# Loading a two-layer megakernel in six waited groups, and moving five pieces of its steady loop

## The reference

```python
# layer 0, on the normalised input
favor:   q, k, v = x@Wq, x@Wk, x@Wv        # 16 heads of 8, 32 random features each
         phi = exp(x @ proj.T - |x|^2/2); causal linear attention; out = num / den
local:   2 blocks of: q, k = l2norm(h@wqkv) * scale, rotary; windowed softmax(q k^T) v; x += o @ wo
         then h = layernorm(shift(x)); x += (a * gelu(g)) @ w2 + b2
# layer 1
attention: 16 heads of 8, softmax(q k^T) v
moe:       top 2 of 8 experts plus a shared one, silu(x@W3) * (x@W1) @ W2
```

## Time and profile before

| | |
|---|---|
| median of 3 runs | 2192.03 us (2189.34 to 2197.23) |
| the profiled execution | 2193.24 us |
| its span in the trace | 2191.5 us |
| mean granted TensorE clock | 0.952 of full |
| first DMA issued / first projection of turn 0 | 8.06 us / 76.48 us |

### The profile page before, as it was taken

One profiled execution on the slowest core, in us unless ns is written; L12 is line 12 of the kernel. 1 busy time (PEld: TensorE's weight loads), 2 busy tenths in 40 slices (PEclk: granted clock), 3 DMA queues, 4 the chain that ended last, 5 costly groups with the idle time before them and its releaser, 6 DMA issues.

```text
span 2191.5 us, 43331 instructions
## 1 busy us (share of the span) xinstructions
PE 1835.0 (84%) x18116; PEld 1061.8 (48%) x18116; DVE 1335.9 (61%) x2752; ACT 765.2 (35%) x1441; POOL 272.2 (12%) x222
## 2 busy tenths in 40 slices
PE   1698898988988889878888888888897988988887
PEld 1254454554544644536445454454553554545544
DVE  1567546765476745767547675476656675467754
ACT  0323433324533235323352232623425223433234
POOL 0101101101021010110210102101011011012010
PEclk9999999999999989999999999999999999999999
DMA  4000200002000020000200001000100002000010
GB/s 177 1 7 2 28 4 6 6 2 30 2 11 1 2 29 6 8 1 2 29 7 7 1 9 23 7 7 1 19 14 6 7 2 29 2 6 1 3 29 7
DMA packets 27477, 29.77 MB, mean 14 GB/s; under 512 B 3525, under 2 KB 25845, under 8 KB 26741
## 3 DMA queue, kind: packets, MB, share of 16 engines
q1 hardware_dynamic: 27284, 27.01, 6.3%
HBM read 12.06 MB, written 2.36 MB: 7 GB/s over the span
## 4 chain that ended last, share of the span: by engine, by line
PE 52%; DVE 28%; ACT 7%; issue 5%; DMA 4%; SPq 4%; POOL 0%; ACTq 0%; DVEq 0%
PE bank L957 5%; PE bank L731 5%; PE bank L947 4%; PE bank L932 4%; DMA phi<-parts 3%; SPq L430 3%; DVE ls L1455 3%; DVE ftm L1381 2%; PE bank L763 2%; PE bank L970 2%; ACT phi L1246 2%; DVE lc L1437 2%; ACT lc L1246 2%; PE bank L669 2%; DVE parts L1391 2%
## 5 line engine op out<-in xcount | busy, mean ns | idle before, releaser
L1622 DVE TENSOR_REDUCE amx<-bank 128x2 f32<-128x512 f32 x256 | 163.1, 685 | 98.4 <-PE bank L970 98.4
L1212 ACT ACTIVATE silu<-bank 128x512 f32<-128x512 f32 x144 | 84.1, 595 | 298.0 <-PE bank L932 286.0
L1610 DVE TENSOR_TENSOR mh<-bank,silu 128x512 f32<-128x512 f32 x144 | 99.5, 692 | 123.4 <-PE bank L947 115.1
L957 PEld LDWEIGHTS bank<-w_mw,mh 128*128 128x128 f32 x1152 | 145.2, 202 | 24.4 <-issue 24.4
L957 PE MATMUL bank<-w_mw,mh 128*128 128x128 f32 x1152 | 153.2, 289 | 0.0
L1641 DVE RECIPROCAL ftm<-bank 128x512 f32<-128x512 f32 x16 | 53.7, 3358 | 154.4 <-PE bank L1053 154.4
L485 POOL TENSOR_TENSOR xB<-xn2T,lsq 128x512 f32<-128x512 f32 x32 | 40.7, 1273 | 812.1 <-ACT lsq L1218 812.1
L932 PE MATMUL bank<-xn2T,w_mw 128*128 128x512 f32 x288 | 141.1, 612 | 0.0
L1455 DVE RECIPROCAL ls<-bank 128x256 f32<-128x256 f32 x64 | 112.2, 1753 | 39.7 <-PE bank L783 39.6
L1443 DVE TENSOR_REDUCE lmx<-bank 128x4 f32<-128x512 f32 x128 | 79.5, 685 | 89.4 <-PE bank L731 89.4
L669 PE MATMUL bank<-hT,w_wqkv 128*128 128x512 f32 x256 | 119.0, 602 | 11.9 <-ACT lsq L1123 6.2
(11 more groups left out here) (284 smaller groups left out, 3678.1 us busy)
## 6 DMA issues: line engine op xcount, KB each, us to landing
phi<-parts SPq DMA_DIRECT2D x96, 64.0 KB
lc<-parts SPq DMA_DIRECT2D x96, 64.0 KB
w_mw<-in_mw SPq DMA_DIRECT2D x3, 1152.0 KB
x_in<-in_x SPq DMA_DIRECT2D x8, 256.0 KB, 2.7
out<-res SPq DMA_DIRECT2D x8, 256.0 KB, 2.3
w_wqkv<-in_wqkv SPq DMA_DIRECT2D x1, 1536.0 KB
w_w<-in_w SPq DMA_DIRECT2D x1, 682.0 KB
mh<-in_rotary SPq DMA_DIRECT2D x1, 512.0 KB
```

The source lines that it names most:

```text
L957: last = mm(bank_of("final")[:, t], mh[:, (2 * q + i) % 4, t], W["mw2"][:, ORDER[q], i, :], start=(q == 0 and j == 0 and i == 0), stop=Fal ...
L1610: V.tensor_tensor(mh[:, n % 4, :], bank_of("moe_u", n)[:], silu[:, n % 2, :], ALU.mult).then_inc(sem["moe_h"], 1)
L1622: V.tensor_reduce(amx[:, 2 * b:2 * b + 2, h], bank_of("att_max", n)[:].rearrange("p (t k) -> p t k", t=2), AX.X, ALU.max).then_inc(sem["at ...
```

## The change

1. SP issues x_in first and then the weights in six groups (LOADS), each with a semaphore of its own; each engine waits for a group where it first needs it. wqkv is loaded in two halves. The 116 first increments go from SP to ACT, in reversed order, and ACT loads its Exp table then. POOL waits for nothing. DVE normalises the first input before it prepares the tables, and PE transposes it before the bias products.
2. EARLY = 3: early values 0 and 1 are computed right after the next turn's input is transposed, early value 2 after the attention's values. In l = 0 only values(3) is left in the turn. In l = 1 values(0) moves in front of sums(0).
3. Quad 7 of the favor attention moves from (1, "raws") to (1, "sums"), its values from (1, "sums") to (1, "nmT").
4. The maxima are dealt out later: pairs 0 and 1 both after expert_out(2), and so on; the last place has one pair instead of two.
5. The centring of l = 0 uses the matrix `center` (identity less 1/128) in place of the mean, ACT squares the bank, and DVE copies it to cen after the square.
6. The denominators of sequence 1: PE multiplies the sums as stationary operand with an 8-column selector (den8), so that they stand transposed in 32 columns; DVE takes 128 x 32 reciprocals, copies them out 16-fold, PE turns them back with four products against the identity (`att_rows`), and DVE multiplies from the bank.

```diff
+LOADS = {
+    "first": ("ident", "cols"),
+    "gated": ("w1", "b1", "center"),
+    "favor": ("fw", "aw", "block8", "projT"),
+    "local": ("rotary", "wqkv0", "rows"),
+    "tables": ("sumrow", "causal", "sumcol", "ident4", "headrow", "winmask", "nmrow", "bandmask", "den", "den8", "mean"),
+    "rest": ("wo", "w2", "wqkv1", "wr", "rb", "pick", "rank", "mw3", "mw1", "mw2"),
 }
...
-        EARLY = 2
+        EARLY = 3
-                    (0, "mean"): 4, (0, "var"): 5, (0, "gain"): 6, (1, "raws"): 7}
+                    (0, "mean"): 4, (0, "var"): 5, (0, "gain"): 6, (1, "sums"): 7}
-                    (0, "var"): 4, (0, "gain"): 5, (0, "out"): 6, (1, "sums"): 7}
+                    (0, "var"): 4, (0, "gain"): 5, (0, "out"): 6, (1, "nmT"): 7}
-        MAX_AT = {3: ((), (0,), (1, 2)), 4: ((3,), (4,), (5,)), 5: ((6,), (7,), (8,)),
-                  6: ((9,), (10,), (11,)), 7: ((12,), (13,), (14, 15))}
+        MAX_AT = {3: ((), (), (0, 1)), 4: ((2,), (3,), (4, 5)), 5: ((6,), (7,), (8,)),
+                  6: ((9,), (10,), (11, 12)), 7: ((13,), (14,), (15,))}
...
         def _(sp):
-            for n in COUNTS:
-                sp.sem_inc(sem[n], COUNTS[n])
+            sp.dma_start(x_in[:], x[0]).then_inc(x_in_sem, 16)
+            for group, names in LOADS.items():
+                for n in names:
...
         def _(pool):
-            pool.wait_ge(loaded, 16 * N_LOADS)
...
+            pe.wait_ge(started, 9)
+            pe.wait_ge(*arrived("first"))
             turn_input(0)
+            bias_products()
             pe.wait_ge(sem["xnT"], COUNTS["xnT"] + 1)
+            pe.wait_ge(*arrived("local"))
             for j in range(EARLY):
                 early_value(0, j)
             pe.wait_ge(sem["loc_v"], COUNTS["loc_v"] + EARLY)
             for i in range(2):
                 favor_query(0, i)
             pe.wait_ge(sem["favor_qk"], COUNTS["favor_qk"] + 2)
+            centred_weights()
             favor_values(0)
+            pe.wait_ge(prep, 13)
+            pe.wait_ge(*arrived("tables"))
...
                         if p == 2:
+                            if l:
+                                values(0)
                             sums(0)
...
                     sums(1)
-                    values(2)
+                    if l:
+                        values(2)
...
-                        mm(o[:], W["mean"][:], h, start=True, stop=True).then_inc(sem["glu_mean_ps"], 1)
+                        mm(o[:], W["center"][:], h, start=True, stop=True).then_inc(sem["glu_mean_ps"], 1)
...
                 if it + 1 < TURNS:
                     turn_input(it + 1)
-                    early_value(it + 1, 0)
+                    for j in range(2):
+                        early_value(it + 1, j)
...
+                        for i in range(4):
+                            last = mm(bank_of("att_pv", b)[:, 8 * i:8 * i + 8], heads[:, b, i * P:(i + 1) * P], W["den8"][:],
+                                      start=True, stop=True)
+                        last.then_inc(sem["att_den"], 1)
+
+                def att_rows():
+                    pe.wait_ge(sem["att_rec"], now("att_rec", 2))
+                    for i in range(4):
+                        last = mm(bank_of("att_pv", 1)[:, i * P:(i + 1) * P], ftm[:, i, :], I[:], start=True, stop=True)
+                    last.then_inc(sem["att_rows_ps"], 1)
...
                 if it + 1 < TURNS:
                     favor_values(it + 1)
-                else:
+                att_rows()
+                if it + 1 == TURNS:
                     att_project(it, 1)
...
         def _(act):
-            act.wait_ge(prep, 14)
+            for n in reversed(COUNTS):
+                act.sem_inc(sem[n], COUNTS[n])
             act.wait_ge(started, 9)
+            A(warm[:], phibias[:], ACT.Exp)
...
+                        if l == 1 and c == 5:
+                            local_value(0)
...
-                        act.wait_ge(sem["glu_cen"], now("glu_cen", l + 1))
-                        A(csq, cen[:], ACT.Square).then_inc(sem["glu_sq"], 1)
+                        act.wait_ge(sem["glu_mean_ps"], now("glu_mean_ps", 1))
+                        A(csq, bank_of("glu_mean", l)[:], ACT.Square).then_inc(sem["glu_sq"], 1)
...
                 A(x1[:].rearrange("p t d -> p (t d)"), bank_of("glu_out", 1)[:], ACT.Copy).then_inc(sem["x1"], 1)
+                if it + 1 < TURNS:
+                    early_value(it + 1, 1)
...
-                        V.tensor_tensor(cen[:].rearrange("p (b t) -> p b t", b=G), hT[:, :, 0:SEQ],
-                                              bank_of("glu_mean", l)[:].rearrange("p (b t) -> p b t", b=G),
-                                              ALU.subtract).then_inc(sem["glu_cen"], 1)
+                        dve.wait_ge(sem["glu_sq"], now("glu_sq", 1))
+                        V.tensor_copy(cen[:], bank_of("glu_mean", l)[:]).then_inc(sem["glu_cen"], 1)
...
+                    else:
+                        link(V.reciprocal(quot[:], bank_of("att_pv", b)[:, 0:32]))
+                        V.tensor_copy(share.rearrange("p (h r) -> p h r", r=16),
+                                      quot[:].unsqueeze(2).broadcast_to([P, 32, 16])).then_inc(sem["att_rec"], 1)
+                        dve.wait_ge(sem["att_rows_ps"], now("att_rows_ps", 1))
+                        V.tensor_tensor(heads[:, b, :], heads[:, b, :], bank_of("att_pv", b)[:], ALU.mult).then_inc(sem["att_o"], 1)
```

More of the change, by code:

```diff
@@ L257, in job @@
         def job(name, k, freed_by, count, ahead=0):
[L258 removed]
+            ring = "late" if (name, k, ahead) == ("loc_v", 2, 1) else ("quad", "wide", "quad", "wide1")[k // 4] if name == "loc_max" else "long" if (name, k) in LONG else RING_OF[name] if name in RING_OF else "short"
             i = RINGS[ring][turns_of[ring] % len(RINGS[ring])]
@@ L287, in build @@
             favor_jobs(l, "raws")
-            for j in range(0 if l else EARLY, TT - 1):
+            for j in range(1 if l else EARLY, TT - 1):
                 job("loc_v", TT * l + j, "loc_v", TT * l + j + 1)
@@ L493, in _ @@
             mm = nc.tensor.matmul
-            pe.wait_ge(loaded, 16 * N_LOADS)
-            pe.wait_ge(prep_ps, 1)
-            for l in range(DEPTH):
-                for c, (o, m) in enumerate(HC):
-                    for g in range(2):
-                        last = mm(bank[0][0:m, 6 * l + 2 * c + g:6 * l + 2 * c + g + 1],
-                                  W["w1"][:, l, g * HID + o:g * HID + o + m], W["cols"][:, 14 + 1 + l:16 + l],
-                                  start=True, stop=True)
@@ L503, in _ @@
-            for i, weights in enumerate((W["fw"], W["aw"])):
-                for side in range(2):
-                    c = 19 + 2 * i + side
-                    last = mm(bank[3][:, i * D:(i + 1) * D], W["cols"][:, c:c + 1].broadcast_to([P, P]), weights[:, 3 + side, :],
-                              start=(side == 0), stop=(side == 1), skip_group_check=True)
-            last.then_inc(prep_ps, 1)
-            pe.wait_ge(prep, 11)
-            for g in range(2):
-                last = mm(bank[1 + g][:, 0:HID], W["center"][:], w1s[:, 1, g * HID:(g + 1) * HID], start=True, stop=True)
@@ L517, in transpose4, with centred_weights @@
+            def centred_weights():
+                pe.wait_ge(prep, 5)
+                for g, o in enumerate((bank_of("xnT"), bank_of("loc_v", 0))):
+                    last = mm(o[:, 0:HID], W["center"][:], w1s[:, 1, g * HID:(g + 1) * HID], start=True, stop=True)
+                last.then_inc(prep_ps, 1)
             def transpose4(o, src, name):
@@ L809, in _ @@
                             loc_pv(k - 1)
+                    if it == 0 and l == 0:
+                        pe.wait_ge(*arrived("rest"))
                     for b in range(G):
@@ L1370, in _ @@
             link(V.memset(ra[:, 0:TT], 1.0))
+            dve.wait_ge(*arrived("first"))
             input_moments(0)
@@ L1374, in _, with made, tables @@
             input_scale(0)
+            done = [0]
+            def made(ins):
+                done[0] += 1
+                ins.then_inc(prep, 1)
+            def tables(l):
+                for qk in range(2):
+                    for i, (trig, half) in enumerate(((0, 0), (1, 1), (0, 1), (1, 0))):
+                        ins = V.tensor_scalar(rot[:, l, qk, i, :], W["rotary"][:, 2 * qk + trig, :],
+                                              W["cols"][:, 2 + 4 * l + 2 * qk + half:3 + 4 * l + 2 * qk + half],
+                                              None, ALU.mult)
+                    made(ins)
@@ new lines, in _ @@
+            made(V.tensor_tensor(projblk[:].rearrange("p (a m) -> p a m", a=4),
+                                 W["projT"].unsqueeze(1).broadcast_to([P, 4, FM]),
+                                 W["block8"].rearrange("p (a m) -> p a m", a=4), ALU.mult))
+            dve.wait_ge(*arrived("local"))
+            tables(0)
+            V.tensor_tensor(b1s[:, :], bank[6][:, 0:12], W["b1"][:], ALU.add)
```

(13 more changed lines are left out.)

141 lines of the change are left out of this document (73 added, 68 removed).

## The result

The changed kernel takes 2121.68 us (median of 4 runs, 2119.54 to 2129.09), the kernel before on the same chip 2191.22 (4 runs, 2189.34 to 2197.23): ratio 0.9692, 95% interval 0.9659 to 0.9726, so 69.5 us less. The forecast was 2108 in a range of 2092 to 2130. The profiled execution has a span of 2119.7 us (before 2191.5), 71.8 less, at a mean granted clock of 0.946 (before 0.952).

What follows compares the result with a forecast made beforehand. PE, busy for 84% of the span, and its hand-overs were taken as the bound. Terms 44.0 + 6.5 + 24 + 13.6 + 1.2 - 5.5 = 83.8 us off 2193.24 gave 2109.4, 2108 as median; range 2092 to 2130.

Steps and rivals of the forecast that it cites:

- the start: Up to the first projection: first issue at 1.5, projection at 32.5 instead of 76.5; 44.0 us gained.
- the denominators: Edge of a turn: 0.6 us in each of seven turns, more in the last; 6.5 us gained (3 to 8).
- the norm: Between the layers: with a second value there PE's clock may hold; half of 0.9 x 7, 3.2 us gained.
- quad 7 and the values: Opening of layer 1: DVE starts 2.0 us earlier, 1.7 a turn net; 13.6 us gained (9 to 16).
- the maxima: At the attention's stacks: L957 is done before the stacks land, in PE's idle; 24 us gained (14 to 28).
- the centring: Layer 0: DVE's copy moves all behind it on DVE by 0.7 us; 5.5 us lost over eight turns.
- the clock's part: At the stacks: 12 us from maxima and gates that ran slowly; two thirds of it, 8, were counted.
- under 3 us of idle: Sign at the stacks: L957 of q = 3 ahead of the first L970, under 3 us idle, 2.05 long.
- the last mask of the maxima waits for the sixth scaling, not the fourth, 0.2: Maxima of layer 1: the banks shift by one, which costs 0.2 us a turn.
- part 4: Opening of layer 1: quad 7 moved later, values(0) and values(1) earlier; 13.6 us gained (9 to 16).
- part 5: Early values: values(2) moves from layer 0 to the norm; 1.2 us gained (2.5 lost to 5 gained).
- the third: Turns bound elsewhere, by the stacks' DMA chain; masks or banks may eat part 4's 1.7; 12 us, 2137; chance 0.15.

Runs made afterwards that it cites:

- e4: The kernel before with only the new start (input first, weights in six groups, clearing and increments moved): 2143.08 us, ratio 0.9788.
- e11: e8 with the change to the denominators of sequence 1 undone too: 2109.78 us, ratio 0.9630.
- e5: The changed kernel with the pairs of maxima back in their old places: 2145.85 us, ratio 0.9782.
- e1: The changed kernel with the ring of short banks turned by one place in layer 1, back to the old banks there: 2120.08 us, ratio 0.9676.
- e2: The changed kernel with two early values instead of three, value 2 back in layer 0: 2109.08 us, ratio 0.9632.
- e3: The changed kernel with quad 7 and values 0 and 1 of layer 1 back in their old places: 2147.13 us, ratio 0.9795.
- e9: e1 with one unread product a turn added in layer 0, where value 2 stood: 2112.80 us, ratio 0.9639.
- e7: The changed kernel, three early values kept, with the short banks of both layers turned back to their old places: 2116.41 us, ratio 0.9646.
- e8: e2 with the centring also back to DVE's subtraction: 2106.68 us, ratio 0.9610.
- e6: The changed kernel with the centring back to the mean product and DVE's subtraction: 2123.69 us, ratio 0.9688.
- e12: The changed kernel with e7's banks, the unread products of e9 and e10, and the centring by DVE's subtraction: 2106.17 us, ratio 0.9587.
- e10: e8 with two unread products a turn added in layer 1 ahead of the transposed roots: 2103.22 us, ratio 0.9606.

## Why the forecast held, and which steps failed

By the stretches of the table the start gave 6.2 us more than its term, the denominators 0.5 and the norm 1.3; quad 7 and the values missed theirs by 12.8, the maxima by 5.3, the centring by 1.7. That is 11.8 short, 83.8 less the table's 72.0 (the other stretches make it 71.8). The turns gave 21.6 us of the 39.8 forecast, so that the time lies well within the range is in part luck: without the extra 6.2 of the start it would have been some 2128.

**Start, right in kind, under-sized.** 50.2 against 44.0. Of the 6.2, 5.0 lie between early value 0 and the first projection (9.1 for 14.1), the price of the values and queries behind the bias products, for which I had taken rows at the lower clock (3.21 instead of 5.7). The rest lies ahead of them, with an issue at 0.74 instead of 1.5. e4 gives 46.5 to 48.3.

**Denominators, right.** 7.0 in the trace, forecast 6.5; the steps measured 0.96, 0.36, 0.43, 1.16 and 0.69. e11 can't tell 4.4 from it.

**Maxima, mechanism right, 24 over-sized.** L991 stands ahead of the stacks in every turn. Two thirds of the clock's part was too much: of the six turns with an idle over 3 us before, the clock held in one, and in two the idle itself didn't shrink. The sign that I had given, under 3 us of idle, failed in five turns of eight. With 0.8 in each of seven turns given back by the query, the net is 18.7; e5 measured 19.7.

**Quad 7 and values, the gain right, its cost mis-sized.** The step "the last mask of the maxima waits for the sixth scaling, not the fourth, 0.2" failed. I had seen the wait (it is the second mask's) and put a sixth of its price on it: nothing hides it, for nothing else is queued ahead of it on PE. It is 1.2 a turn, and with the longer stretch at the lower clock 14.6 in all (e1: 15.5 came back). And it wasn't part 4's: it goes when part 5 alone is undone (e2) and stays when part 4 is (e3). The ring hands out banks in the order of the jobs; part 4 moves jobs within l = 1, part 5 takes one away in l = 0, and that shifts all that follow.

**Early values, the wrong sign.** Forecast 1.2 gained; undoing the part gave 13 us (e2). The norm's gain is there, 3.4 in all, against 3.2 forecast. (The term itself has a slip: 3.2 with 0.1 a turn gained and 0.3 lost is 1.6.) Against it stand the shift above and the stand in l = 0, which I had booked at 0.1 gained: value 2 was the cover of ACT's copy, and with its 1.0 us of work PE kept its clock. e9 puts an unread product in its place: there the clock falls at the sums in no turn instead of five, and the median is 8 us lower. How much of e2's 13 is which can't be read off, as e7 lies between.

**Centring, right in e2's surroundings** (4.8 in e8, forecast 5.5), invisible in the changed kernel (e6), where the same 8.3 us went to the clock elsewhere.

**Clock.** Of the rivals, the third had the shifted banks eat the gain of part 4, and so it came; but its stacks' chain and its 12 us for the turns did not. Beside that came the last condition of the forecast, "if the clock falls somewhere new". The trace of before had 0.952, that of after 0.946. At 1.2 GHz for (1 - clock) x 2 of the span that is 210 and 229 us. What such a microsecond costs can be estimated from runs of one kernel: in e9 2104.94 us at 0.953 and 2119.33 at 0.941, 14.4 us for 52 us more at the lower level, 0.28 each; in e12 it is 27.1 for 52. The 19 us more in the changed kernel are then, as an estimate, some 5 to 10 of the 14 that are missing; they lie in the stretches counted above, not beside them. The fall moves with each edit, and its sum with each run. The Trainium skill (TensorE: Matmul & The Clock Gate, "Part 1: The HAM clock gate") says that what watches PE's activity runs free of the kernel. The traces fit that, since the same stand of 0.81 us has the fall beside it in two turns of the changed kernel, in none of e5 and in seven of e3; no run here shows it by itself. Why it falls behind one stand of 0.8 us and not behind the next stays open.

## What to carry to other kernels

Where banks are handed out in turn, count the jobs: one job taken away in one layer changes who waits for whom in all that follow, and a wait that appears on an engine with nothing else to do costs its full length. Before moving work out of an idle place, ask what it covered: PE's stand and its clock behind it are part of its price. With a clock like this, read an edit's effect in its own stretch of the trace and in the median; here the two differed by 5 to 14 us (e1: 15.5 and 1.6; e3: 10.4 and 22.6; e6: 8.3 and none; e10: 6.4 and 0.9).

## What was not expected of the hardware

Behind an idle of 0.81 us PE ran at 1.2 GHz, in e1's turn 2 for over 20 us (0.50 from 567.4 to 588.0), though PE was busy for 18.89 of the 20.60 us of that window; and with 1.0 us of unread work in that idle (e9) the clock didn't fall there in any turn and the median was 8 us lower. In e1 and e6 what was won in one stretch (15.5 and 8.3 us) was lost in others, in which no instruction differs.
